# Four consecutive tokens to a partition, and another order of the work in front of the experts

## What is computed

```python
x = x + gat(ctx, adj=layernorm(x))      # two layers, 8 heads of 64, elu after each
xf = layernorm(x)
scores = softmax(xf @ gate_w.T); w, idx = top_k(scores, 6)
# each expert takes at most 128 of its tokens, in the order of the token numbers
gu = xf[tokens] @ gate_up[e]; hid = silu(gu[:192]) * gu[192:]
out[tokens] += (hid @ down[e]) * w
out += (silu(xf @ shared_gate.T) * (xf @ shared_up.T)) @ shared_down.T
x = x + out
```

## Time and profile before

| | |
|---|---|
| median of 3 runs | 708.5 us (704.78 to 715.64) |
| profiled execution | 706.73 us, its span 705.0 us |
| mean granted clock of PE | 0.919 |
| PE busy | 584.1 us (83%) |
| DVE, ACT, POOL busy | 230.0, 173.0, 246.5 us |
| DMA | 141.44 MB, 201 GB/s over the span |

### The profile page before, as it was taken

How to read it: one execution, slowest core, us unless ns; L and a number is a source line. 1 busy time by engine, 2 the same in 40 slices (tenths; PEclk the granted TensorE clock), 3 DMA queues, 4 the chain that set the end, 5 groups by cost and what they waited for, 6 DMA issues and landing times.

```text
span 705.0 us, 6326 instructions
## 1 busy us (share of the span) xinstructions
PE 584.1 (83%) x2035; PEld 312.2 (44%) x2035; DVE 230.0 (33%) x572; ACT 173.0 (25%) x352; POOL 246.5 (35%) x235
## 2 busy tenths in 40 slices
PE   5999827777799999999999997999789998964810
PEld 2444314554445555555555553555345554532400
DVE  3866724863832222222132221222212222220210
ACT  4577733365101111121111111111011121110100
POOL 1145573353141333343323424333233333324220
PEclk9999959778989999999999999999979999996965
DMA  8935434489134989999998897997968898987432
GB/s 231 242 131 105 42 109 158 170 257 280 60 108 132 272 222 272 251 268 268 248 263 230 223 261 202 263 262 218 255 158 252 245 269 267 241 208 198 101 45 34
DMA packets 68953, 141.44 MB, mean 201 GB/s; under 512 B 13553, under 2 KB 16113, under 8 KB 68913
## 3 DMA queue, kind: packets, MB, share of 16 engines
q1 hardware_dynamic: 48240, 93.22, 42.7%
q0 software_dynamic: 18032, 43.54, 30.2%
q10 hardware_dynamic: 2640, 4.20, 1.7%
HBM read 107.89 MB, written 33.04 MB: 200 GB/s over the span
## 4 chain that ended last, share of the span: by engine, by line
DMA 43%; PE 28%; issue 12%; DVE 5%; ACT 4%; POOL 4%; SPq 1%; POOLq 0%; ACTq 0%; DVEq 0%
DMA out<-y,table 38%; PE bank L773 8%; PE bank L652 6%; PE bank L761 5%; DMA out<-x 5%; PE bank L666 3%; PE bank L575 2%; ACT rows L844 1%; PE bank L753 1%; SPq L319 1%; POOL picked L416 1%; DVE ones_lo L1082 1%; POOL x L425 1%; DVE ones_hi L1078 1%; DVE s L1003 1%
## 5 line engine op out<-in xcount | busy, mean ns | idle before, releaser
L501 POOL DMA_INDIRECT out<-y,table x64 | 101.4, 1584 | 294.8 <-DMA out<-y,table 213.2
L773 PE MATMUL bank<-gu_w,gxT 128*128 128x384 f32 x512 | 176.6, 488 | 0.8 <-ACT gxT L945 0.8
L761 PE MATMUL bank<-dn_w,hidT 96*128 96x512 f32 x256 | 126.7, 618 | 1.0 <-DVE hidT L1216 1.0
L1199 DVE TENSOR_SCALAR y<-bank,gx 128x512 f32<-128x512 f32 x64 | 48.1, 751 | 225.1 <-PE bank L761 208.9
L773 PEld LDWEIGHTS bank<-gu_w,gxT 128*128 128x128 f32 x512 | 93.0, 192 | 52.2 <-issue 1.6
L953 ACT ACTIVATE eg<-bank 128x192 f32<-128x192 f32 x64 | 21.2, 331 | 287.5 <-PE bank L773 287.5
L652 PE MATMUL bank<-xnT,upT 128*128 128x512 f32 x192 | 91.3, 620 | 0.0
L1211 DVE TENSOR_TENSOR hid<-bank,eg 128x192 f32<-128x192 f32 x64 | 31.8, 497 | 130.1 <-ACT eg L953 130.1
L753 PE MATMUL bank<-ident,gx 128*128 128x128 f32 x256 | 40.9, 284 | 36.9 <-DMA gx<-rows_dram,table 36.9
L507 POOL DMA_INDIRECT gx<-rows_dram,table x64 | 63.6, 994 | 21.7 <-issue 18.9
L761 PEld LDWEIGHTS bank<-dn_w,hidT 96*128 96x128 f32 x256 | 47.7, 197 | 48.5 <-issue 47.1
(11 more groups left out here) (164 smaller groups left out, 464.9 us busy)
## 6 DMA issues: line engine op xcount, KB each, us to landing
gu_w<-in_gate_up SPq DMA_DIRECT2D x128, 384.0 KB, 4.3
dn_w<-in_down SPq DMA_DIRECT2D x128, 192.0 KB, 5.8
x<-in_x SPq DMA_DIRECT2D x4, 1024.0 KB, 9.3
feat_dram<-feat SPq DMA_DIRECT2D x16, 256.0 KB, 3.1
rows_dram<-rows ACTq DMA_DIRECT2D x4, 1024.0 KB, 4.8
out<-x SPq DMA_DIRECT2D x4, 1024.0 KB, 5.7
out<-x POOLq DMA_DIRECT2D x3, 1024.0 KB, 10.4
w<-in_W SPq DMA_DIRECT2D x5, 256.0 KB, 7.7
```

Source lines behind the costliest of these rows:

```text
L501: pool.indirect_dma_start(a["out"][:, :], bass.IndirectOffsetOnAxis(ap=table[:, e:e + 1], axis=0), y[:, e % YB, :], None, compute_op=ALU.a ...
L761: last = nc.tensor.matmul(DN[:], hidT[:, e % 2, j, :], dn_w[:, e % U, j, :], start=(j == 0), stop=(j == 1))
L773: last = nc.tensor.matmul(GU[e % 2][:, 0:2 * I], gxT[:, e % 2, c, :], gu_w[:, e % U, c, :], start=(c == 0), stop=(c == KC - 1))
L1199: nc.vector.tensor_scalar(y[:, e % YB, :], DN[:], gx[:, e % GX, D + e:D + e + 1], None, ALU.mult).then_inc(y_ready, 1)
```

## The change

Token b·512 + 4p + t now lies in partition p: a partition holds four consecutive tokens, in loads, stores and tables alike. So the numbers of a batch are one run of 16 bytes per partition (128 runs) where they were 512 runs of 4 bytes. `place` needs the ranks in token order: it takes three products with `upto` and three with `strict` instead of three with `eighth`. The hidden index of the first layer is permuted the same way, W1 comes by one DMA in pieces of 1 KB (four DMAs with pieces of 256 bytes before), W0 and b1 by ACT's queue. `store_node` moves to SP's queue, and stands between the stores of tiles. `norm` is called by the tile and reads its input in order, writing it in strides (before it read in strides). The rest moves instructions. The table gives the same list of tokens.

```diff
+
+                def store_node(b):
+                    sp.wait_ge(node_ready, b + 1)
+                    sp.dma_start(a[f"node_dram{b}"].rearrange("(p t) u -> p (t u)", t=TB),
+                                 node[:, b * TB:(b + 1) * TB]).then_inc(node_stored[b % 2], 16)
+
+                def store_feat(n):
+                    b, t = n // TB, n % TB
+                    sp.wait_ge(z2_ready, n + 1)
+                    sp.dma_start(a[f"feat_dram{b}"].rearrange("(p t) d -> p t d", t=TB)[:, t, :], feat[:, t, :]).then_inc(feat_out[t], 16)
...
-                    sp.dma_start(a["out"][b * N:(b + 1) * N, :].rearrange("(t p) d -> p t d", p=P),
+                    sp.dma_start(a["out"][b * N:(b + 1) * N, :].rearrange("(p t) d -> p t d", t=TB),
...
-                             a["W0"].rearrange("h f o -> f h o")).then_inc(w0_in, 16)
+                sp.dma_start(w1[:].rearrange("p h c o -> p h (c o)"),
+                             a["W1"].rearrange("h (p c) o -> p h (c o)", c=KC)).then_inc(w1_in, 16)
                 load_nodes(1)
                 load_x(0)
...
-                store_feat(0)
-                store_feat(1)
-                store_feat(2)
-                store_feat(3)
+                store_node(0)
+                for n in range(NT):
+                    store_feat(n)
+                    if n in node_after:
+                        store_node(node_after[n])
...
-                store_node(0)
                 node_of_node(0)
-                store_node(1)
                 node_of_node(1)
-                store_node(2)
                 pick(0)
                 add(0)
                 node_of_node(2)
                 scale(0)
-                store_node(3)
                 pick(1)
                 add(1)
                 node_of_node(3)
                 scale(1)
                 pick(2)
                 add(2)
-                pool.wait_ge(sq_ready, 1)
-                nc.gpsimd.tensor_tensor(sumsq[:], sumsq[:], k.mhalf[:], ALU.pow).then_inc(sq_rstd, 1)
                 scale(2)
+                pick(3)
                 count_seen(0)
-                pick(3)
                 weigh(0)
                 count_seen(1)
                 scale(3)
                 weigh(1)
+                pool.wait_ge(sq_ready, 1)
+                nc.gpsimd.tensor_tensor(sumsq[:], sumsq[:], k.mhalf[:], ALU.pow).then_inc(sq_rstd, 1)
                 count_seen(2)
                 weigh(2)
...
+                    if n == 0:
+                        pe.wait_ge(w1_in, 16)
...
-                    if n == 3 * TB:
-                        for t in range(TB):
-                            xn_turn(t)
-                    if n == 3 * TB + 1:
+                    if n in (3 * TB, 3 * TB + 1):
+                        xn_turn(2 * t)
+                        xn_turn(2 * t + 1)
+                    if n == 3 * TB + 2:
                         gate(0)
...
-                unit(0)
                 gate(1)
                 invert(0)
                 for t in range(TB):
                     xn_turn(2 * TB + t)
-                unit(1)
+                unit(0)
                 place(1)
                 gate(2)
                 invert(1)
-                unit(2)
                 invert_rest()
+                unit(1)
                 for t in range(TB):
...
-                unit(4)
+                unit(2)
                 place(3)
-                unit(5)
+                unit(3)
...
-                for u in range(6, units):
+                for u in range(4, units):
                     unit(u)
...
-                        nc.scalar.activation(rows[:, b % 2, t, :].rearrange("q (c p) -> q c p", c=KC),
-                                             k.x[:, n, :].rearrange("q (p c) -> q c p", c=KC), ACT.Identity,
-                                             scale=k.rstd[:, n:n + 1], bias=shift[:, b % 2, t:t + 1]).then_inc(xn_ready, 1)
...
+                    nc.scalar.activation(rows[:, b % 2, t, :].rearrange("q (c p) -> q p c", c=KC),
+                                         k.x[:, n, :].rearrange("q (p c) -> q p c", c=KC), ACT.Identity,
+                                         scale=k.rstd[:, n:n + 1], bias=shift[:, b % 2, t:t + 1]).then_inc(xn_ready, 1)
...
-                        squares(t)
+                        squares(2 * t)
+                        squares(2 * t + 1)
...
-                    if b == 2:
-                        squares(3 * TB + t)
-                        if t == 0:
...
-                            act.wait_ge(turn_done, turn[("nodes", B - 1)] + 1)
-                            nc.scalar.activation(nodes[:], nodes[:], ACT.Abs).then_inc(abs_nodes, 1)
-                        if t == TB - 1:
-                            norm(0)
+                        squares(2 * TB + 2 * t)
+                        squares(2 * TB + 2 * t + 1)
+                    if n == 2 * TB + 2:
+                        norm(0)
+                    if n == 2 * TB + 3:
+                        norm(1)
...
+                        copy_xn(1)
+                    if n == 3 * TB + 1:
+                        copy_xn(2)
+                        copy_xn(3)
+                        store_rows(0)
+                        nc.scalar.activation(nodes[:], nodes[:], ACT.Abs).then_inc(abs_nodes, 1)
+                    if n == 3 * TB + 2:
+                        norm(TB)
+                        norm(TB + 1)
...
+                act.wait_ge(small_in, 80)
+                for j in range(4):
...
                 silu(0, 0)
-                gate_exp(1)
-                silu(0, 1)
-                norm(3)
+                for t in range(TB):
+                    norm(3 * TB + t)
                 turned(3)
                 gate_exp(2)
+                silu(0, 1)
                 gate_exp(3)
                 silu(0, 2)
...
-                for t in range(TB):
-                    largest(t)
+                    largest(c)
...
-                    if n == 2 * TB + 1:
+                    if n == 2 * TB:
                         moments(0)
-                    if n == 3 * TB - 1:
+                    if n == 3 * TB + 2:
                         dve.wait_ge(abs_nodes, 1)
                         nc.vector.tensor_reduce(rowstat[:, 0:1], nodes[:].rearrange("p t f -> p (t f)"),
                                                 AX_X, ALU.max).then_inc(abs_nodes, 1)
+                    if n == 3 * TB:
                         moments(1)
+                        dve.wait_ge(squared, NT)
+                        nc.vector.tensor_scalar(sumsq[:], sumsq[:], 1.0 / D, EPS, ALU.mult, ALU.add).then_inc(sq_ready, 1)
                 elu2(NT - 1)
                 choose(0)
                 moments(2)
                 split(0)
-                dve.wait_ge(squared, NT)
-                nc.vector.tensor_scalar(sumsq[:], sumsq[:], 1.0 / D, EPS, ALU.mult, ALU.add).then_inc(sq_ready, 1)
                 choose(1)
                 add(3)
...
-                shared_up(0, 1)
                 choose(3)
...
+                shared_up(0, 1)
```

More of the change, by code:

```diff
@@ L605, in place @@
                     for t in range(TB - 1):
[L606 to L608 removed]
+                        nc.tensor.matmul(POS[:, (t + 1) * E:TB * E], k.upto[:],
+                                         mine[:, t:t + 1, :].broadcast_to([P, TB - 1 - t, E]), start=False, stop=False)
+                    for t in range(1, TB):
+                        last = nc.tensor.matmul(POS[:, 0:t * E], k.strict[:],
+                                                mine[:, t:t + 1, :].broadcast_to([P, t, E]), start=False, stop=(t == TB - 1))
                     last.then_inc(pos_done, 1)
@@ new lines, in _, with turned @@
+                    if n == 3 * TB + 1:
[6 more added lines that the diff above has]
+                        norm(TB + 1)
+                norm(TB + 2)
+                norm(TB + 3)
+                def turned(b):
+                    for t in range(TB):
+                        copy_xn(b * TB + t)
+                    store_rows(b)
@@ L920, in _ @@
                 turned(1)
                 gate_exp(0)
-                norm(2)
+                for t in range(TB):
+                    norm(2 * TB + t)
                 turned(2)
+                act.wait_ge(small_in, 80)
+                for j in range(4):
+                    nc.scalar.activation(small[:, j, :], small[:, j, :], ACT.Abs,
+                                         accum_out=bounds[:, 3 + j:4 + j]).then_inc(abs_small, 1)
+                nc.scalar.activation(small[:, 4, :], small[:, 4, :], ACT.Abs).then_inc(abs_small, 1)
@@ L924, in _ @@
+                gate_exp(1)
                 silu(0, 0)
-                gate_exp(1)
-                silu(0, 1)
-                norm(3)
+                for t in range(TB):
+                    norm(3 * TB + t)
                 turned(3)
                 gate_exp(2)
+                silu(0, 1)
                 gate_exp(3)
```

105 lines of the change are left out of this document (47 added, 58 removed).

## The result

Over 20 runs each the changed kernel took 706.6 us (median) and the kernel before 709.6, a ratio of 0.9942 with a 95% interval of 0.9916 to 0.9968. The forecast was 692, its range 681 to 704. So the change gains half a per cent, where two were expected. Ratios are taken from fast executions alone, those within 1.5% of the fastest of their kernel, so they are not the quotients of the medians, which are over all.

The account below looks back on a forecast made before the run. The prediction took a dependent line through five engines ahead of an unchanged experts' stage of 494.95 us as the bound. First turning 14.5 us earlier: 705.0 - 14.5 = 690.5, plus 1.73 outside the span, 692; range 681 to 704.

Parts of the forecast that it names:

- Start, +1.2: Tile 0's start: x(0) behind W1 and searches between first-layer chunks put the first `s` at 23.5 instead of 22.31 us.
- the 26 that I had set as a sign of being wrong: Upper bound for the first `s`, with x(0) at 16 us; coming later would show the prediction wrong.
- Loop: Tile loop: second squares in tiles 0 to 3 add 2.4 us to tile 8; loop's end gains 10, `choose(0)` at 111.3.
- Node numbers: Node-number writes and picks: write takes 2.6 us, first lands hidden at 40; pick(1)'s adds begin 5.7 us after issue.
- A rival had the picks still at 11 us: Picks of gathered batches stay late because engines behind the queues are what they wait for; 694 us, chance 0.05.
- `choose(0)` to the table, 63.1: Routing stretch on DVE: its own 55.0 us plus remaining or new waits make 63.1 instead of 75.7, gaining 12.5.
- a rival at 0.07: Routing: another wait replaces POOL's 20.77 us, say PE at low clock throughout, and the line keeps 75.7; 704.5, chance 0.07.
- POOL's power: POOL's 20.77 us wait ahead of `scale(2)` goes, so scale ends at 120.0, was 139.1; the last pick's 5.9 wait goes.
- Units, +7.8: Behind the table: two `half_up` units of 3.5 us and an uncovered evacuation of 0.8 move there, adding 7.8 us.
- Strides in norm, 0: ACT's normalised tiles: strided writes instead of strided reads, about 1.2 us each, taken at no gain.
- Three copies, 0: Final chain: `add_shared` copies with 8 KB runs instead of 2 KB, bounds -14 to +6 us for three, taken as 0.
- the 0.15 left out: Chance of falling outside 681 to 704: outer ends of the copies' bounds, and the rivals at 704.5 and slower.

Follow-up runs that it names:

- w0_on_sp: The changed kernel with W0 issued on SP's queue behind nodes(0) again, no longer on ACT's; ratio to the kernel before 0.9761.
- The filling: The changed kernel with products nobody uses added on PE, five ahead of gate(1), three each ahead of gates 2 and 3; ratio to the kernel before 0.9809.
- The third order: The changed kernel with W0 on SP's queue and PE's units 0 to 2 ahead of gates 1 to 3, 3 and 4 around place(3), five behind the table; ratio 0.9602.
- adds_later: The third order, W0 on SP, with POOL's adds of batch 0 held until the `s` of tile 7; ratio to the kernel before 0.9672.
- after: The changed kernel itself as first profiled, against the kernel before; 706.6 us median, ratio 0.9942.

## Why the prediction was wrong

**Start, +1.2: wrong, +7.4.** The step failed where I took the input bytes as one stream at the rate of the first slices, "there at 13.2 us". That sum leaves out who is served. The engines were quicker than I took them (328 GB/s), and W1 and x(0) held up nothing; W0, at the head of ACT's queue beside 8.8 MB of SP's, took 15.5. The first `s` at 29.75 is past the 26 that I had set as a sign of being wrong. With W0 back on SP the first `s` came at 22.5 to 25.5 in six runs, inside the bounds 21 to 26, and there the search stands for x(0) as I had it: DVE was held until 13.76 in w0_on_sp.

**Loop: right in sum, not in its parts.** +2.4 to tile 8 was +5.1: the squares' own 2.4 are borne out to tile 4, and tile 4's products at the low clock, 1.9, were not in the sum. The way from tile 8 to `choose(0)` was 39.8 us instead of 42.6; 2.2 of that lie between the `s` of tiles 11 and 12, which followed after 1.7 us where I had 3.9. The 87.8 predicted and 87.7 measured owe their likeness to two errors that cancel.

**Node numbers: right at the pick, wrong at the first write.** The adds of batch 1 began 5.3 us after the pick (92.68 after 87.41). The first write did not wait for the loads until 40: issued at 28.58, it let the gathers start at 30.55. It was hidden either way. The write took 1.9 us; for the 2.6 that I took no row was shown. A rival had the picks still at 11 us. The Trainium skill (DMA: Bandwidth & Descriptors, on issuing engines that are not separate DMA queues) says that issuing on several engines saves issue time only. For this write the runs agree: on either queue the adds began 5.0 to 5.3 us after the pick, and shortening it did all. For W0 the queue did matter, as above.

**`choose(0)` to the table, 63.1: wrong, 69.8.** "DVE's own 55.0" held (54.7). The waits were 15.1 instead of 8.1: 4.5 at `topc`, for which I had nothing; 5.9 instead of 4.0 at the shared product, as its unit (4.7 us instead of 3.5) and the inverting before it (1.9 instead of 1.1) ran in part at the low clock; 2.9 instead of 1.5 at `place(3)` behind a unit; 1.8 instead of 1.0 at `spare`; the 1.6 for `place(1)` and the last table did not show. I took each PE piece at its length of before and only asked what stood ahead of it in the queue. But what I moved were the products that had brought PE back to its high clock: before the change the units in front of the gates took 4.54, 5.67 and 5.25 us, where a unit at the high clock takes 3.6, and the gates behind them 3.7. The change took `unit(0)` from in front of gate(1) and left 3.84 us of waiting there. I had this as half of a rival at 0.07 ("PE at the low clock all through the routing"): with the other waits it took back 6.7 of the 12.5 us that the step forecast. The filling alone returned 3.15 us of it; that the rest is the clock's is read from the lengths of the pieces, not from a run. The third order, which puts a unit ahead of each gate and none behind `invert_rest`, took 16.9 us less than the kernel before.

**POOL's power: right that the wait goes.** The 5.9 us at the last pick went with it, but alone it gave 3.7 us of the 12.5, since `spare` and `cross` grew by 2.8; the rest hung on PE's order. The new order without POOL's edit was not run.

**Units, +7.8: right.** Table to first turning rose by 7.76 us.

**Strides in norm, 0: right.** The sixteen tiles took 1.23 to 1.30 us (median 1.26), before 1.27 to 1.30. **Three copies, 0: right within the noise**; their median landing was 10.9 us, before 10.4.

**The range.** Its terms of 2.5 for the start and 3 for the experts were honest for each, but the two errors had one sign and both were causes I had named, one as a bound and one as a rival at 0.07. That they could come together was not in the 0.15 left out.

## What to carry to other kernels

When products are moved on PE, ask what they did for the ones behind them: a piece that is used as filling in front of a short, waited-for product can be worth more there than its own length, and the best order tried here puts one in front of each. When a load changes its queue, ask what is outstanding on the others, since a sum of bytes over the bandwidth gives the end of the last one and not of the one that is waited for. Take away one wait at a time and look for the next before adding up gains: here POOL's edit alone gave 3.7 us, and with the whole change and the third order on PE it was 16.9.

## What the runs showed of the hardware

A quarter of a megabyte with 8.8 MB issued on another queue landed 15.5 us after issue in one run, and PE's first layer behind it began between 14.5 and 20.0 us in the five runs with that order; with 2.6 MB on the other queue it took 10.6.

A wait of the same length had two outcomes. PE stood 3.35 us ahead of tile 4 in the changed kernel and ran the next products at 5.41 us; it stood 3.34 us there in adds_later and ran them at 3.60, on PE's timeline:

```profile
40.96 1.25 PE L570 MATMUL bank<-ctxT,w 128*128 128x512 f32 x2 [3.34 <-ACT ctxT L801]
42.05 3.60 PE L582 MATMUL bank<-w,h1T 128*128 128x512 f32 x8
```

Likewise, in the five runs with the changed kernel's own order on PE, gate(2) took between 3.75 and 6.68 us, while gates 1 and 3 took 7.06 in each. Ahead of gate(3) in the changed kernel the clock was 1.00 from 156.95 to 159.30 us, while PE turned tiles, and 0.50 from 161.80 on, behind a wait of 2.52 us and through the short f16 products of `place`. When the clock falls was not settled here.

DVE waited on POOL: an elu with both operands in SBUF took 2.64, 1.42 and 1.63 us beside POOL's adds in three runs (w0_on_sp, after, adds_later), 0.69 without them. The Trainium skill (SBUF — State Buffer, on who interferes with whom) says that a DVE instruction with two SBUF inputs contends with a GpSimd instruction that reads SBUF, and that the later one waits for the whole of the other. The rows agree in part: holding the adds back took the 2 us away. But the elu of 2.64 us began at 55.12, beside the first of two adds in a row, and ended 0.6 us behind the second (57.20), so it stood for longer than that one instruction.
